# Variance products in groups of four slots, a ring of 18 slots of units, and sums and later layers one slot later, in a fused graph-network kernel

## The chip, the cores and the metric

The kernel runs on one core of a Trainium2 chip, in one launch. The metric is the time of the launch on the device in microseconds (us). Lower is better. Three runs of the kernel before took 2769.07, 2771.56 and 2772.95 us.

The core has a matrix engine (PE, whose weight loads the profile lists as PEld), a vector engine (DVE, VectorE), an activation engine (ACT, ScalarE), a general engine (POOL, GpSimd) and a queue engine that starts DMAs (SP). They run side by side and meet only at semaphores.

## The reference, cut to what matters

64 independent graphs of 128 nodes with 128 features go through four layers. All numbers are float32. Nearly all the work is layer 0, which makes a hidden vector for each of the 128 x 128 pairs of nodes:

```
hi = x @ W1[:H];  hj = x @ W1[H:]
h = relu(hi[:, None, :] + hj[None, :, :] + b1)      # 128 x 128 pairs, 128 numbers each
y = h @ W2 + b2
y = (y - mean(y)) / sqrt(var(y) + 1e-5) * gamma + beta
out[i] = sum over j of adj[i, j] * y[i, j]
```

The later layers (a normalized graph convolution, a sum with a two-matrix network, and three convolutions with layer norms) work on one 128x128 matrix per graph, each a product or two and a norm.

## The kernel before

**Layer 0.** A unit is 128 pairs: h for one i, features on the partitions, j along the free dimension. Eight units are a slot's worth (`DUO_UNITS`), and a graph has 16 of them (`SLOTS`). A slot's worth t goes through these steps:

- hidden (L547, L662, L917): the eight units `relu(v + u_i)`, shared out over three engines. DVE makes unit 0 where t is odd (four units where t is 15), POOL the last two or three, ACT what is between.
- products (L403): two PE products of 128x512 with the centred W2, into one of two halves of `y_ps`. The first needs units 0 to 3 and, through `sq_done`, that the half is free; the second needs the rest.
- squares (L565): ACT reads both halves' 1024 columns, squares them and writes `sq`, a ring of `SQ_RING` = 4 slots.
- variances (L419): PE sums squares over the features. A product with a shifted one-column selector (`sel`) writes 32 rows of `ss_ps`, and four such products (q = 0 to 3, two slots' worth of two blocks) go to four groups of 32 columns of the array.
- deviations (L569): once per half graph (eight slots' worth) ACT takes the square root of `ss_ps`. SP straightens it into `devs` with four narrow DMAs, DVE inverts it and multiplies it into the adjacency (`invert` L689, `coefficients` L694), SP stores that to DRAM and reads it back spread over the partitions (`cb`).
- weighted sums (L673): DVE multiplies each unit of h by its coefficients and sums, eight per slot's worth. The buffer `h` holds 16 slots' worth, and a hidden step waits until the sum 16 slots earlier is done (`ttr_done`).

**The order.** It is written by hand. Every engine runs an endless pipeline of iterations (one per graph) of 16 slots, and in slot s it works on the slot's worth s minus a lag:

```
hidden: s - START (START = 4)        products: s - (START + 1)
squares: s - (START + 2)             variances: s - (START + 3), at odd s
deviations: START + HALF + 2 = 14    invert, coefficients: START + HALF + 3 = 15
weighted sums: first half of the eight at s - TTR_LAG = s - 18, second at s - 19
```

So in slot n PE multiplies n-5, while ACT first squares n-6 and then makes the units of n-4. PE's order in a slot is: first product, later-layer steps of places 0 to 3, second product, later-layer steps of places 4 to 8, variance products. ACT's is: square, deviations where due, later-layer steps of places 1 to 3, units (with steps of places 4 to 7 after the second and the fourth unit), the rest. POOL makes its last unit a slot ahead (`EARLY_AT`), and makes three units in the slots of `ROOTLESS`, those in which no root of a norm falls on it.

**Later layers.** The table `AT` (L88) gives each step of the later layers a slot and a place within it. The steps of a graph are spread over some 29 slots behind its layer 0, in the iterations of the next graphs (`tails`). SP's order per iteration stands in `iteration` (L361), and each of its waits holds up what is behind it.

Of the kernel before, what the change touches and what calls it, by code (L numbers as in the profile page):

```python
# [20 lines left out]
START = 4  # L21
TTR_LAG = START + 14
TAIL_LAG = START + 28
LAYERS = 3
SQ_RING = 4
ROOTLESS = (1, 2, 4, 6, 8, 10, 13, 15)
SPAN = P // 2
# [60 lines left out]
for _name, _slot, _fine in [  # L88
    ("adj_turn", 0, 0), ("adj_turned", 0, 6), ("row_sum", 0, 2), ("degree", 0, 5), ("has_degree", 1, 5),
    ("c_sum_mm", 1, 4), ("c_sum", 1, 8), ("x_base", 2, 3),  # L90
# [9 lines left out]
]:  # L100
    place(_name, _slot, _fine)


def build(nc, x, adj, nodemask, l0_W1, l0_b1, l0_W2, l0_b2, l0_gamma, l0_beta, l1_W, l1_b,
# [4 lines left out]
    with ExitStack() as ctx:  # L109
# [39 lines left out]
        uT, vT = sb("uT", [P, 2, P]), sb("vT", [P, 2, P])  # L149
        h = sb("h", [P, SLOTS, DUO_UNITS * P])  # L150
        sq = sb("sq", [P, SQ_RING, DUO_UNITS * P])
# [125 lines left out]
        def _(sp):  # L277
# [83 lines left out]
            def iteration(after, graphs, buf):  # L361
                new, old, older, oldest = graphs
                if old is not None:
                    spread_coefficients(old, 0)
                if after is not None:
                    wait_apart(sp, x_turned, new + 1)
                    wait_apart(sp, x_in_in, 16 * (new + 1))
                    sp.dma_start(x_in[:], x[after]).then_inc(x_in_in, 16)
                if old is not None:
                    straighten_deviations(old, 1)  # L370
                    store_coefficients(old, 1)
                    spread_coefficients(old, 1)
                    if new is not None:
                        load_adj_c(new)
                    load_tail(old, 1 - buf)
                if oldest is not None:
                    wait_apart(sp, normed["ln3"], oldest + 1)
                    wait_apart(sp, out_stored, 16 * oldest)
                    sp.dma_start(out[oldest], x4[:, 1 - buf, :]).then_inc(out_stored, 16)
                if new is not None:  # L380
                    straighten_deviations(new, 0)
                    store_coefficients(new, 0)
# [5 lines left out]
        def _(pe):  # L388
# [15 lines left out]
            def products(g, t, block_of_duo):  # L404
# [10 lines left out]
                c0 = block_of_duo * COLS  # L415
                op = pe.matmul(y_ps[:, t % 2, c0:c0 + COLS], w2c[:], h[:, t, c0:c0 + COLS], start=True, stop=True)  # L416
                if block_of_duo == 1:
                    op.then_inc(y_done, 1)

            def variances(g, t):  # L420

                half, p = t // HALF, (t % HALF) // 2
                wait(pe, sq_done, SLOTS * g + t + 2)
                if p == 0:
                    wait(pe, dev_done, 2 * g + half)
                for q in range(4):
                    c0 = (q % 2) * COLS
                    mm = pe.matmul(ss_ps[32 * q:32 * q + 32, :], sel[:, ROWS - 1 - p:ROWS - 1 - p + 32],  # L428
                                   sq[:, (t + q // 2) % SQ_RING, c0:c0 + COLS],
                                   start=(p == 0), stop=(p == ROWS - 1))  # L430
                mm.then_inc(var_summed, 1)
# [75 lines left out]
            def iteration(after, graphs, buf):  # L507
                new = graphs[0]
                for s in range(SLOTS):
# [11 lines left out]
                    for g, b, place in tails(graphs, buf, s):  # L521
                        later_layers(g, b, place + 4, place + FINE)
                    if s == 11 and after is not None:
                        turn_x(after, 1 - buf)
                    sg, t = lagging(graphs, s, START + 3)
                    if s % 2 == 1 and sg is not None:
                        variances(sg, t)
# [4 lines left out]
        def _(act):  # L532
# [14 lines left out]
            def hidden(g, b, t, n):  # L547

                if n == vector_units(g, t):
                    wait(act, ttr_done, SLOTS * (g - 1) + t + 1)  # L550
                    if t == 0:
                        wait(act, uv_ready, g + 1)
                i = unit_of(t, n)
                v = v_ps if t < SLOTS - 1 else vT[:, b, :]
                op = act.activation(h[:, t, n * P:(n + 1) * P], v, ACT.Relu, bias=uT[:, b, i:i + 1])  # L555
                if n == BLOCK_UNITS - 1:
# [4 lines left out]
            def squares(g, t):  # L561

                wait(act, y_done, SLOTS * g + t + 1)
                wait(act, var_summed, SLOTS // 2 * g + (t - SQ_RING) // 2 + 1)
                act.activation(sq[:, t % SQ_RING, :], y_ps[:, t % 2, :], ACT.Square,  # L565
                               bias=b2c_col[:], scale=float(P) ** -0.5).then_inc(sq_done, 1)

            def deviations(g, half):

                wait(act, var_summed, SLOTS // 2 * g + HALF // 2 * (half + 1))  # L570
                wait(act, devs_in[half], 64 * g)
# [44 lines left out]
            def iteration(after, graphs, buf):  # L616
                new = graphs[0]
                for s in range(SLOTS):
# [31 lines left out]
                    if act_end(hg, ht) <= first + 4:  # L650
                        tail_steps(6, 8)
                    if s == 12 and after is not None:
                        keep_xT(after, 1 - buf)
# [5 lines left out]
        def _(dve):  # L659
            def hidden(g, b, t, n):  # L660

                if n == 0:  # L662
                    wait(dve, ttr_done, SLOTS * (g - 1) + t + 1)
                    if t <= 1:
                        wait(dve, uv_ready, g + 1)

                i = unit_of(t, n)
                op = dve.tensor_scalar(h[:, t, n * P:(n + 1) * P], vT[:, b, :], uT[:, b, i:i + 1], 0.0, ALU.add, ALU.max)  # L668
                if n == vector_units(g, t) - 1:
                    op.then_inc(h_dve, 1)  # L670

            def weighted_sum(g, t, n):

                if n == 0:
# [4 lines left out]
                    if t == 0:  # L679
# [3 lines left out]
                c0 = (t % 2) * DUO_UNITS * P + n * P  # L683
                op = dve.tensor_tensor_reduce(h[:, t, cols], h[:, t, cols], cb[:, t // 2, c0:c0 + P],  # L684
                                              1.0, 0.0, ALU.mult, ALU.add, gT[:, i:i + 1])
# [187 lines left out]
        def _(pool):  # L873
# [43 lines left out]
            def hidden(g, b, t, n):  # L917

                wait(pool, ttr_done, SLOTS * (g - 1) + t + 1)
                if t == 0:  # L920
                    wait(pool, uv_ready, g + 1)
                i = unit_of(t, n)
                op = pool.tensor_scalar(h[:, t, n * P:(n + 1) * P], vT[:, b, :], uT[:, b, i:i + 1], 0.0, ALU.add, ALU.max)  # L923
                if n == DUO_UNITS - 1:
# [44 lines left out]
```

## Time and profile before

| what | value |
|---|---|
| median of the runs shown | 2771.56 us (2769.07 to 2772.95) |
| profiled execution, its own time | 2773.57 us |
| its span, first to last instruction | 2772.0 us |
| mean granted clock of PE | 0.989 of full speed |
| PE busy | 2707.0 us, 98% |
| DVE busy | 2618.7 us, 94% |
| ACT busy | 2565.2 us, 93% |
| POOL busy | 2491.0 us, 90% |
| DMA | mean 206 GB/s, queue busy 54.5% |

How to read it. The times of one profiled execution are set against its own time, which is 1.6 us above its span. Engines overlap, so busy shares do not add up. A product shows as two passes (MATMUL rows "x2"), each with a weight load (LDWEIGHTS). Matmuls are pipelined and their ends are modelled, so starts are compared with starts, and a row's length is longer than its distance to the next row. The timeline merges neighbours of one kind into one row: its columns are start, length, engine, line, operation, and in brackets the idle time of the engine before it with what ended it. "issue" is time in which nothing in the profile was waited for.

### The profile page before, as it was taken

The page shows a single profiled execution, that of the slowest core. Times are in us where ns is not written, and L with a number is a line of the kernel's source. Part 1 is how long each engine was busy: PE and PEld are TensorE (multiplying, and loading weights), DVE is VectorE, ACT ScalarE, POOL GpSimd, SP SyncE. Part 2 cuts the span into 40 slices and gives each one's busy share as a digit, 9 for nine tenths or more (in the row PEclk, how much of TensorE's full clock was granted, in tenths as well). Part 3 has the DMA queues.
Part 4 walks back from the last instruction along what each step waited for, and adds up shares of the span by engine and source line. Part 5 has one row for each costly group of instructions (what it writes and reads, how often), then busy time and mean ns, then how long its engine had stood idle before and what let it go on. Part 6 is the DMA issues. An engine that isn't in the chain of part 4 may idle for free.

```text
span 2772.0 us, 60903 instructions
## 1 busy us (share of the span) xinstructions
PE 2707.0 (98%) x10882; PEld 1128.4 (41%) x10882; DVE 2618.7 (94%) x20102; ACT 2565.2 (93%) x6903; POOL 2491.0 (90%) x3498
## 2 busy tenths in 40 slices
PE   8999999999999999999999999999999999999993
PEld 2344444444444444444444444444444444444442
DVE  4999999999999999999999999999999999999997
ACT  7999999999999999999999999999999999999991
POOL 3899999999999999999999999999999989999992
PEclk9999999999999999999999999999999999999995
DMA  3655655655555555556556555555555565465552
GB/s 104 239 195 211 234 198 197 230 215 192 214 226 202 204 216 222 195 213 234 195 198 235 209 192 227 223 193 210 226 207 195 205 234 203 192 228 222 193 214 108
DMA packets 188668, 571.72 MB, mean 206 GB/s; under 512 B 70656, under 2 KB 106368, under 8 KB 139136
## 3 DMA queue, kind: packets, MB, share of 16 engines
q1 hardware_dynamic: 188288, 567.83, 54.5%
q14 instruction: 285, 2.33, 0.2%
q8 instruction: 95, 1.56, 0.2%
HBM read 555.17 MB, written 8.39 MB: 203 GB/s over the span
## 4 chain that ended last, share of the span: by engine, by line
PE 59%; DVE 13%; ACT 11%; DMA 10%; issue 5%; SPq 2%; POOL 0%; DVEq 0%; POOLq 0%; ACTq 0%
PE y_ps L416 41%; PE ss_ps L428 11%; DVE h L684 8%; ACT h L555 6%; DMA cb<-c_scratch 6%; ACT sq L565 3%; DMA c_scratch<-c 2%; DMA devs<-dev_rows 2%; SPq L324 1%; ACT dev_rows L572 1%; PE prod_bank L478 1%; PE prod_bank L482 1%; DVE h L668 1%; DVE stats L708 1%; DVE gT L684 1%
## 5 line engine op out<-in xcount | busy, mean ns | idle before, releaser
L923 POOL TENSOR_SCALAR h<-vT,uT 128x128 f32<-128x128 f32 x2520 | 2063.8, 834 | 54.1 <-ACT vT L545 44.6
L684 DVE CUSTOM_DVE_ANT_0 h<-h,cb 128x128 f32<-128x128 f32 x8192 | 2005.8, 291 | 74.4 <-DMA cb<-c_scratch 71.4
L416 PE MATMUL y_ps<-h,w2c 128*128 128x512 f32 x4096 | 2032.8, 613 | 11.9 <-DVE h L668 2.8
L555 ACT ACTIVATE h<-uv_ps,uT 128x128 f32<-128x128 f32 x4785 | 1426.9, 441 | 0.0
L565 ACT ACTIVATE sq<-y_ps,b2c_col 128x1024 f32<-128x1024 f32 x1024 | 1193.5, 1166 | 139.3 <-PE y_ps L416 138.6
L416 PEld LDWEIGHTS y_ps<-h,w2c 128*128 128x128 f32 x4096 | 672.9, 190 | 944.1 <-issue 647.3
L684 DVE DVE_READ_ACCUMULATOR2_ANT gT<- 128x1 f32 x8192 | 637.5, 78 | 0.0
L428 PE MATMUL ss_ps<-sq,sel 128*32 128x512 f32 x4096 | 545.5, 605 | 0.8 <-ACT sq L565 0.8
L914 POOL TENSOR_TENSOR rs<-var_eps,minus_half 128x1 f32<-128x1 f32 x448 | 297.9, 665 | 35.1
L911 POOL TENSOR_TENSOR var_eps<-mv,eps_col 128x1 f32<-128x1 f32 x448 | 94.8, 212 | 132.7 <-DVE mv L711 129.2
L668 DVE TENSOR_SCALAR h<-vT,uT 128x128 f32<-128x128 f32 x757 | 202.1, 295 | 4.7 <-ACT mask_all L610 2.6
L428 PEld LDWEIGHTS ss_ps<-sq,sel 128*32 128x32 f32 x4096 | 80.6, 108 | 247.8 <-ACT sq L565 141.2
L708 DVE BATCH_NORM_STATS2 stats<-z 128x6 f32<-128x128 f32 x448 | 127.1, 284 | 0.3
L482 PEld LDWEIGHTS prod_bank<-l3w,aggT 128*128 128x128 f32 x384 | 73.4, 193 | 93.3 <-issue 73.0
L692 DVE RECIPROCAL invs<-devs 128x64 f32<-128x64 f32 x128 | 70.2, 548 | 38.4 <-DMA devs<-dev_rows 36.7
L717 DVE TENSOR_SCALAR x<-z,mv,rs 128x128 f32<-128x128 f32 x256 | 96.7, 378 | 6.1 <-POOL rs L914 4.8
L603 ACT ACTIVATE h<-z_aff 128x128 f32<-128x128 f32 x192 | 75.7, 394 | 19.0 <-DVE z_aff L791 19.0
L711 DVE BATCH_NORM_AGGREGATE mv<-stats 128x2 f32<-128x6 f32 x448 | 78.4, 175 | 4.7
L572 ACT ACTIVATE dev_rows<-ss_ps 128x512 f32<-128x512 f32 x128 | 79.6, 622 | 1.2 <-PE ss_ps L428 1.2
L598 ACT ACTIVATE aggT<-prod_bank 128x128 f32<-128x128 f32 x192 | 61.6, 321 | 20.6 <-PE prod_bank L478 20.6
L482 PE MATMUL prod_bank<-l3w,aggT 128*128 128x128 f32 x384 | 76.3, 281 | 2.6 <-ACT aggT L598 2.6
L791 DVE SCALAR_TENSOR_TENSOR z_aff<-z_aff,rs,l3beta 128x128 f32<-128x128 f32 x192 | 75.0, 391 | 3.0 <-POOL rs L914 3.0
(100 smaller groups left out, 1460.6 us busy)
## 6 DMA issues: line engine op xcount, KB each, us to landing
cb<-c_scratch SPq DMA_DIRECT2D x384, 1024.0 KB, 9.4
cb<-c_scratch SPq DMA_DIRECT2D x256, 512.0 KB, 4.9
adj_c<-in_adj_dram SPq DMA_DIRECT2D x512, 8.0 KB
devs<-dev_rows SPq DMA_DIRECT2D x512, 8.0 KB
x_in<-in_x_dram SPq DMA_DIRECT2D x64, 64.0 KB, 10.9
c_scratch<-c SPq DMA_DIRECT2D x128, 32.0 KB, 1.5
adj_in<-in_adj_dram SPq DMA_DIRECT2D x64, 64.0 KB, 4.4
x_res<-in_x_dram SPq DMA_DIRECT2D x64, 64.0 KB, 5.3
```

The costliest lines, as they stand in the source:

```text
L416: op = pe.matmul(y_ps[:, t % 2, c0:c0 + COLS], w2c[:], h[:, t, c0:c0 + COLS], start=True, stop=True)
L428: mm = pe.matmul(ss_ps[32 * q:32 * q + 32, :], sel[:, ROWS - 1 - p:ROWS - 1 - p + 32], sq[:, (t + q // 2) % SQ_RING, c0:c0 + COLS], start= ...
L482: pe.matmul(out, aggT[:, b, :], l3w[:, i, :], start=True, stop=False)
L555: op = act.activation(h[:, t, n * P:(n + 1) * P], v, ACT.Relu, bias=uT[:, b, i:i + 1])
L565: act.activation(sq[:, t % SQ_RING, :], y_ps[:, t % 2, :], ACT.Square, bias=b2c_col[:], scale=float(P) ** -0.5).then_inc(sq_done, 1)
L572: act.activation(dev_rows[:, half, :], ss_ps[:], ACT.Sqrt, bias=EPS).then_inc(dev_done, 1)
L668: op = dve.tensor_scalar(h[:, t, n * P:(n + 1) * P], vT[:, b, :], uT[:, b, i:i + 1], 0.0, ALU.add, ALU.max)
L684: op = dve.tensor_tensor_reduce(h[:, t, cols], h[:, t, cols], cb[:, t // 2, c0:c0 + P], 1.0, 0.0, ALU.mult, ALU.add, gT[:, i:i + 1])
L708: dve.bn_stats(stats[:, b, :], z[:, b, :]).then_inc(stats_set[name], 1)
L717: dve.tensor_scalar(dst[:, b, :], z[:, b, :], mv[:, b, 0:1], rs[:, b:b + 1], ALU.subtract, ALU.mult).then_inc(normed[name], 1)
L914: pool.tensor_tensor(rs[:, b:b + 1], var_eps[:, b:b + 1], minus_half[:], ALU.pow).then_inc(rs_set[name], 1)
L923: op = pool.tensor_scalar(h[:, t, n * P:(n + 1) * P], vT[:, b, :], uT[:, b, i:i + 1], 0.0, ALU.add, ALU.max)
```

## The change

Four things change together.

- A variance step takes four slots' worth (`GROUP` = 4), eight products instead of four, and stands in slots 1, 5, 9 and 13 instead of in every odd slot. The ring of squares goes from 4 to 6, and the waits on `var_summed` count groups of four.
- `h` becomes a ring of 18 slots' worth (`H_RING`), and the weighted sums come one slot later (`TTR_LAG` = START + 15). A hidden step waits for the sum 18 slots earlier.
- All steps of the later layers from `g_keep` on, the transposition of the next x and its copy are placed one slot later. `ROOTLESS`, the slots in which POOL makes three units, follows the places of the roots.
- SP starts the narrow DMAs of the first half's deviations before the store of the output instead of after it.

```diff
-TTR_LAG = START + 14
-TAIL_LAG = START + 28
+TTR_LAG = START + 15
+H_RING = 18
 LAYERS = 3
-SQ_RING = 4
-ROOTLESS = (1, 2, 4, 6, 8, 10, 13, 15)
+SQ_RING = 6
+GROUP = 4
+ROOTLESS = (1, 2, 3, 5, 7, 9, 11, 14)
...
-    ("g_keep", 2, 4), ("l0_mm", 3, 0), ("l0_sum", 3, 5), ("ln0", 3, 6), ("x1_scaled", 4, 6),
-    ("l1_agg", 5, 0), ("l1_agg_keep", 5, 8), ("l1_mm", 6, 0), ("l1_bias", 6, 7), ("l1_relu", 7, 0),
+    ("g_keep", 3, 4), ("l0_mm", 4, 0), ("l0_sum", 4, 5), ("ln0", 4, 6), ("x1_scaled", 5, 6),
+    ("l1_agg", 6, 0), ("l1_agg_keep", 6, 8), ("l1_mm", 7, 0), ("l1_bias", 7, 7), ("l1_relu", 8, 0),
...
-    ("l3_relu2", 26, 6), ("final_sum", 28, 2), ("ln3", 28, 3),
+    ("l3_relu2", 27, 6), ("final_sum", 29, 2), ("ln3", 29, 3),
...
-        h = sb("h", [P, SLOTS, DUO_UNITS * P])
+        h = sb("h", [P, H_RING, DUO_UNITS * P])
...
+                if new is not None:
+                    straighten_deviations(new, 0)
                 if oldest is not None:
                     wait_apart(sp, normed["ln3"], oldest + 1)
                     wait_apart(sp, out_stored, 16 * oldest)
                     sp.dma_start(out[oldest], x4[:, 1 - buf, :]).then_inc(out_stored, 16)
                 if new is not None:
-                    straighten_deviations(new, 0)
                     store_coefficients(new, 0)
...
             def variances(g, t):
 
-                half, p = t // HALF, (t % HALF) // 2
-                wait(pe, sq_done, SLOTS * g + t + 2)
-                if p == 0:
+                half = t // HALF
+                wait(pe, sq_done, SLOTS * g + t + GROUP)
+                if t % HALF == 0:
                     wait(pe, dev_done, 2 * g + half)
-                for q in range(4):
-                    c0 = (q % 2) * COLS
-                    mm = pe.matmul(ss_ps[32 * q:32 * q + 32, :], sel[:, ROWS - 1 - p:ROWS - 1 - p + 32],
-                                   sq[:, (t + q // 2) % SQ_RING, c0:c0 + COLS],
-                                   start=(p == 0), stop=(p == ROWS - 1))
+                for d in range(GROUP):
+                    p = (t + d) % HALF // 2
+                    for block in range(2):
+                        q = 2 * (d % 2) + block
+                        mm = pe.matmul(ss_ps[32 * q:32 * q + 32, :], sel[:, ROWS - 1 - p:ROWS - 1 - p + 32],
+                                       sq[:, (SLOTS * g + t + d) % SQ_RING, block * COLS:(block + 1) * COLS],
+                                       start=(p == 0), stop=(p == ROWS - 1))
                 mm.then_inc(var_summed, 1)
...
-                    if s == 11 and after is not None:
+                    if s == 12 and after is not None:
                         turn_x(after, 1 - buf)
-                    sg, t = lagging(graphs, s, START + 3)
-                    if s % 2 == 1 and sg is not None:
+                    sg, t = lagging(graphs, s, START + 1 + GROUP)
+                    if t % GROUP == 0 and sg is not None:
                         variances(sg, t)
...
-                    wait(act, ttr_done, SLOTS * (g - 1) + t + 1)
+                    wait(act, ttr_done, SLOTS * g + t - H_RING + 1)
...
-                wait(act, var_summed, SLOTS // 2 * g + (t - SQ_RING) // 2 + 1)
-                act.activation(sq[:, t % SQ_RING, :], y_ps[:, t % 2, :], ACT.Square,
+                wait(act, var_summed, (SLOTS * g + t - SQ_RING) // GROUP + 1)
+                act.activation(sq[:, (SLOTS * g + t) % SQ_RING, :], y_ps[:, t % 2, :], ACT.Square,
...
-                    if s == 12 and after is not None:
+                    if s == 13 and after is not None:
                         keep_xT(after, 1 - buf)
```

The index of `h` becomes `(SLOTS * g + t) % H_RING` wherever it is read or written, and DVE's and POOL's hidden steps wait as ACT's does.

**PE, from the round of slot 5 to that of slot 7 in the steady stretch, before.** The names: y_ps are layer 0's products (two per slot), ss_ps the variance products, prod_bank the later layers. The first row is the round of slot 5, the last the round of slot 7.

```order
L428 MATMUL ss_ps<-sq,sel 32x512 x4
L416 MATMUL y_ps<-h,w2c 128x512
L463 MATMUL prod_bank<-l1wT,aggT 128x128
L416 MATMUL y_ps<-h,w2c 128x512 x2
L478 MATMUL prod_bank<-adj_in,h 128x128
L416 MATMUL y_ps<-h,w2c 128x512
L428 MATMUL ss_ps<-sq,sel 32x512 x4
```

The same place in the changed kernel, from the round of slot 5 towards that of slot 9:

```order
L432 MATMUL ss_ps<-sq,sel 32x512 x8
L418 MATMUL y_ps<-h,w2c 128x512
L464 MATMUL prod_bank<-adjT,x1s 128x128
L418 MATMUL y_ps<-h,w2c 128x512 x2
L467 MATMUL prod_bank<-l1wT,aggT 128x128
L418 MATMUL y_ps<-h,w2c 128x512 x2
L482 MATMUL prod_bank<-adj_in,h 128x128
L418 MATMUL y_ps<-h,w2c 128x512 x2
L486 MATMUL prod_bank<-l3w,aggT 128x128
L487 MATMUL prod_bank<-bias_parts,pick 128x128
```

Before, four layer 0 products lie between two rounds. After, eight do, with the later layers' products of four slots between them (the last layer 0 product, the two products of l2_agg and the round follow the listing).

**SP, from the narrow loads of one graph to the store of its first coefficients, before.**

```order
L288 DMA adj_c<-in_adj_dram 32x1x64 x8
L358 DMA adj_in<-in_adj_dram 128x128
L359 DMA x_res<-in_x_dram 128x128
L379 DMA out_dram<-x 128x128
L324 DMA devs<-dev_rows 32x1x64 x4
L335 DMA c_scratch<-c 128x64
```

And after:

```order
L289 DMA adj_c<-in_adj_dram 32x1x64 x8
L359 DMA adj_in<-in_adj_dram 128x128
L360 DMA x_res<-in_x_dram 128x128
L325 DMA devs<-dev_rows 32x1x64 x4
L382 DMA out_dram<-x 128x128
L336 DMA c_scratch<-c 128x64
```

The output's store now stands between the deviations' narrow DMAs and the store of the coefficients made from them.

## Rows read from the trace of the kernel before

**Rows 1.** The page: busy time by engine, and shares of the last chain.
```profile
PE 2707.0 (98%) x10882; PEld 1128.4 (41%) x10882; DVE 2618.7 (94%) x20102; ACT 2565.2 (93%) x6903; POOL 2491.0 (90%) x3498
PE 59%; DVE 13%; ACT 11%; DMA 10%; issue 5%; SPq 2%; POOL 0%; DVEq 0%; POOLq 0%; ACTq 0%
```

**Rows 2.** Timeline of PE, the row of L401 in two graphs.
```profile
298.39 0.38 PE L401 MATMUL uv_ps<-xT,w1a 128*128 128x128 f32 x2
...
2365.55 0.39 PE L401 MATMUL uv_ps<-xT,w1a 128*128 128x128 f32 x2
```

**Rows 3.** Timeline of PE from 1399.5 us.
```profile
1399.52 1.02 PE L416 MATMUL y_ps<-h,w2c 128*128 128x512 f32 x2
1400.38 0.38 PE L460 MATMUL prod_bank<-adjT,x1s 128*128 128x128 f32 x2
1400.60 1.02 PE L416 MATMUL y_ps<-h,w2c 128*128 128x512 f32 x2
1401.55 1.07 PE L428 MATMUL ss_ps<-sq,sel 128*32 128x512 f32 x8
1402.55 1.12 PE L416 MATMUL y_ps<-h,w2c 128*128 128x512 f32 x2
1403.51 0.38 PE L463 MATMUL prod_bank<-l1wT,aggT 128*128 128x128 f32 x2
```

**Rows 4.** Timeline of PE, the four small passes ahead of a round.
```profile
1390.19 0.50 PE L449 MATMUL prod_bank<-rows_sum,row_pick 128*128 128x1 f32 x4
1390.63 1.07 PE L428 MATMUL ss_ps<-sq,sel 128*32 128x512 f32 x8
```

**Rows 5.** Timeline of PE, the product that waited for ACT, and one later.
```profile
1404.87 1.12 PE L416 MATMUL y_ps<-h,w2c 128*128 128x512 f32 x2
1405.83 0.38 PE L478 MATMUL prod_bank<-adj_in,h 128*128 128x128 f32 x2
...
1408.96 0.39 PE L482 MATMUL prod_bank<-l3w,aggT 128*128 128x128 f32 x2
1409.18 0.22 PE L483 MATMUL prod_bank<-bias_parts,pick 96*128 96x128 bf16 x1
1409.24 1.07 PE L416 MATMUL y_ps<-h,w2c 128*128 128x512 f32 x2
1410.15 0.38 PE L466 MATMUL prod_bank<-adj_in,x 128*128 128x128 f32 x2
```

**Rows 6.** Timeline of ACT over the same stretch.
```profile
1403.13 0.65 ACT L572 ACTIVATE dev_rows<-ss_ps 128x512 f32<-128x512 f32 x1
1403.61 1.20 ACT L555 ACTIVATE h<-uv_ps,uT 128x128 f32<-128x128 f32 x4
...
1405.06 1.22 ACT L565 ACTIVATE sq<-y_ps,b2c_col 128x1024 f32<-128x1024 f32 x1
1406.05 1.51 ACT L555 ACTIVATE h<-uv_ps,uT 128x128 f32<-128x128 f32 x5
1407.30 0.43 ACT L598 ACTIVATE aggT<-prod_bank 128x128 f32<-128x128 f32 x1
...
1410.36 1.11 ACT L565 ACTIVATE sq<-y_ps,b2c_col 128x1024 f32<-128x1024 f32 x1 [0.34 <-PE y_ps L416]
```

**Rows 7.** Timeline of PE's weight loads: a round, and the product that waited.
```profile
1401.55 0.16 PEld L428 LDWEIGHTS ss_ps<-sq,sel 128*32 128x32 f32 x8 [0.76 <-ACT sq L565]
...
1404.86 0.30 PEld L416 LDWEIGHTS y_ps<-h,w2c 128*128 128x128 f32 x2 [0.94 <-ACT h L555]
```

**Rows 8.** Waits by engine and line: us in total, times, longest us.
```profile
PEld y_ps L416 <- ACT h L555: 198.3, 383, 1.5
...
PEld y_ps L416 <- DVE h L668: 81.0, 93, 1.9
...
DVE h L684 <- DMA cb<-c_scratch: 71.4, 116, 2.7
...
DVE invs L692 <- DMA devs<-dev_rows: 36.7, 48, 19.8
```

More of the change, by code:

```diff
@@ L415, in products @@
                 c0 = block_of_duo * COLS
-                op = pe.matmul(y_ps[:, t % 2, c0:c0 + COLS], w2c[:], h[:, t, c0:c0 + COLS], start=True, stop=True)
+                op = pe.matmul(y_ps[:, t % 2, c0:c0 + COLS], w2c[:], h[:, (SLOTS * g + t) % H_RING, c0:c0 + COLS], start=True, stop=True)
                 if block_of_duo == 1:
@@ L554, in hidden @@
                 v = v_ps if t < SLOTS - 1 else vT[:, b, :]
-                op = act.activation(h[:, t, n * P:(n + 1) * P], v, ACT.Relu, bias=uT[:, b, i:i + 1])
+                op = act.activation(h[:, (SLOTS * g + t) % H_RING, n * P:(n + 1) * P], v, ACT.Relu, bias=uT[:, b, i:i + 1])
                 if n == BLOCK_UNITS - 1:
@@ L563, in squares @@
                 wait(act, y_done, SLOTS * g + t + 1)
-                wait(act, var_summed, SLOTS // 2 * g + (t - SQ_RING) // 2 + 1)
-                act.activation(sq[:, t % SQ_RING, :], y_ps[:, t % 2, :], ACT.Square,
+                wait(act, var_summed, (SLOTS * g + t - SQ_RING) // GROUP + 1)
+                act.activation(sq[:, (SLOTS * g + t) % SQ_RING, :], y_ps[:, t % 2, :], ACT.Square,
                                bias=b2c_col[:], scale=float(P) ** -0.5).then_inc(sq_done, 1)
             def deviations(g, half):
-                wait(act, var_summed, SLOTS // 2 * g + HALF // 2 * (half + 1))
+                wait(act, var_summed, SLOTS // GROUP * g + HALF // GROUP * (half + 1))
                 wait(act, devs_in[half], 64 * g)
@@ L662, in hidden @@
                 if n == 0:
-                    wait(dve, ttr_done, SLOTS * (g - 1) + t + 1)
+                    wait(dve, ttr_done, SLOTS * g + t - H_RING + 1)
                     if t <= 1:
@@ L667, in hidden @@
                 i = unit_of(t, n)
-                op = dve.tensor_scalar(h[:, t, n * P:(n + 1) * P], vT[:, b, :], uT[:, b, i:i + 1], 0.0, ALU.add, ALU.max)
+                op = dve.tensor_scalar(h[:, (SLOTS * g + t) % H_RING, n * P:(n + 1) * P], vT[:, b, :], uT[:, b, i:i + 1], 0.0, ALU.add, ALU.max)
                 if n == vector_units(g, t) - 1:
@@ L683, in weighted_sum @@
                 c0 = (t % 2) * DUO_UNITS * P + n * P
-                op = dve.tensor_tensor_reduce(h[:, t, cols], h[:, t, cols], cb[:, t // 2, c0:c0 + P],
+                op = dve.tensor_tensor_reduce(h[:, (SLOTS * g + t) % H_RING, cols], h[:, (SLOTS * g + t) % H_RING, cols], cb[:, t // 2, c0:c0 + P],
                                               1.0, 0.0, ALU.mult, ALU.add, gT[:, i:i + 1])
@@ L917, in hidden @@
             def hidden(g, b, t, n):
-                wait(pool, ttr_done, SLOTS * (g - 1) + t + 1)
+                wait(pool, ttr_done, SLOTS * g + t - H_RING + 1)
                 if t == 0:
@@ L922, in hidden @@
                 i = unit_of(t, n)
-                op = pool.tensor_scalar(h[:, t, n * P:(n + 1) * P], vT[:, b, :], uT[:, b, i:i + 1], 0.0, ALU.add, ALU.max)
+                op = pool.tensor_scalar(h[:, (SLOTS * g + t) % H_RING, n * P:(n + 1) * P], vT[:, b, :], uT[:, b, i:i + 1], 0.0, ALU.add, ALU.max)
                 if n == DUO_UNITS - 1:
```

12 rows, old and new, of the table AT are left out of this document.

## The prediction

> **What bounds the kernel now.** I read the page first [rows 1]. Four engines are busy for 90 to 98% of the span, so no busy share names the bound, and the chain of waits puts 59% on PE. The period comes next. PE makes u and v (L401) once per graph, and two such rows 49 graphs apart give (2365.55 - 298.39) / 49 = 42.19 us per graph [rows 2]. The 64 graphs make 2700 us of it; the rest is filling and draining.
>
> Then PE's timeline [rows 3]. A 128x512 product is two passes. From L416 at 1399.52 to L460 at 1400.38 is 0.86, so a pass is 0.43 and a slot's two products take 1.72. From L416 at 1400.60 to the variance products at 1401.55 is 0.95, 0.09 more than two passes. A round of four variance products lasts 1.00 to the next product, and that product takes 0.96, again 0.10 more. A round costs 0.09 + 1.00 + 0.10 = 1.19 us, and it stands after every second slot: eight per graph. A 128x128 product costs 0.22 (L460 to L416), l3w with its bias product 0.28 (1408.96 to 1409.24), and the four small L449 passes 0.35, being 0.44 less the entry's 0.09 [rows 3 to 5].
>
> Last, how PE and ACT hold each other. PE's slot n makes the product of unit-slot n-5, while ACT in slot n squares n-6 and then makes units of n-4. The second last pass of a product begins at 1409.24 and its last 0.43 before L466 at 1410.15, at 1409.72; the waiting square starts at 1410.36, 0.64 later [rows 5, 6]. From the square at 1405.06 to the next ACT unit is 0.99, and five units take 1.25, 0.25 each [rows 6]. The units that start at 1403.61 have their fourth at 1404.36, and the product that waited for it starts at 1404.87, 0.50 later; its weight loads stand at the same moment with "ACT h" behind them, and it takes 0.96 to the next row, 0.10 more than a stream [rows 5 to 7].
>
> So there is a two-slot loop. With P(n) the start of PE's slot n and A(n) the start of ACT's square: A(n) is at least P(n-1) + 1.29 + 0.63 = P(n-1) + 1.92 plus what stands between the two products, and P(n+1) is at least A(n) + 1.01 + three pitches 0.75 + 0.50 = A(n) + 2.26. In odd slots VectorE makes the first unit, and it is A(n) + 2.01. The loop is **3.9 to 4.2 us over two slots**, and small ACT steps or a late ACT come on top. Of the 42.19, 16 x 1.72 and 8 x 1.19 are products and rounds; 5.2 is left for later layers and waits, about 0.3 per slot. So PE without a round needs 2.0 a slot, while ACT needs 1.0 + four to six units at 0.25 + small steps, 2.0 to 2.7. Today every two slots hold one round and last 5.2, which covers both the loop and ACT nearly everywhere; PE waits for ACT's units at one slot, 1404.87, behind the deviations at 1403.13 [rows 6, 7].
>
> **The change part by part.** *Groups of four.* Four rounds of eight replace eight rounds of four. The same products are made, and a round of eight has four streams of passes in place of two. In a round of four, 1.00 is the last pass with its change (0.52, as 0.95 less 0.43) and 0.48 for the first four passes [rows 3]. Two more streams cost 0.86 to 0.96; I take 0.90. A round of eight is then 0.09 + 1.90 + 0.10 = 2.09, against 2.38 for two rounds: **PE has 0.29 less per pair, 256 x 0.29 = 74 us over the kernel.** The bounds: nothing, if each further stream pays entry and exit again (0.19 + 0.10 and the stagger), and 0.33.
>
> The weight loads could take that gain. All eight loads of a round start within 0.16 us of its beginning, though its passes last 1.00 [rows 7], so loads for the second stream lie under the first, and I charge none. The Trainium skill, "TensorE: Matmul & The Clock Gate", section "What overlaps and what doesn't", says weight loads overlap running matmuls only when their row groups differ; here all four tiles use all 128 rows, so by it each further stream would pay its load. At the loads' 0.11 that would be 0.21 per round of eight, 54 us over the kernel. The trace speaks against that rule for this form, and the sum goes without it.
>
> *Where the cover goes.* Rounds now stand behind slots 1, 5, 9 and 13 only. I step P and A through a graph; a product behind a round or a wait takes 1.82. Slots 6 to 9, with P(6) = 0: round 5 has just ended. ACT squared long ago, but its deviations need the round's last pass (0.52 earlier, seen 0.63 after its start), so they begin at 0.11 and take 0.48 [rows 6]. Six units and a copy follow, and A(7) = 2.25. P(7) = 1.82 + 0.22 = 2.04, no wait. P(8) by PE would be 3.98, but A(7) + 2.01 = 4.26. A(8) = 2.25 + ACT's slot 7 (1.0 + four units 1.0 + 0.2) = 4.45, so P(9) is 6.71 where PE by itself says 4.26 + 1.82 + 0.22 = 6.30. Then P(10) = 6.71 + 1.82 + later layers 0.73 + the round's 1.99 = 11.25. By the same steps slots 10 to 13 take 10.76 (waits at 12 and 13), slots 14 to 1 take 10.68 (waits at 0 and 1) and slots 2 to 5 take 10.44 (nearly no wait, since slot 3's later-layer work has moved to slot 4). **The sum is 43.13 us per graph, 0.94 above today's 42.19.** PE's work falls by 4 x 0.29 = 1.2, but some six waits a graph take its place, 0.2 to 0.5 each with 0.10 behind them. Over 64 graphs that is +60 us.
>
> *Ring of 18, sums one slot later.* VectorE waits 71.4 us for coefficients (cb) and 36.7 for deviations [rows 1, 8]. One slot more removes most of the first. That is worth nothing on the path: VectorE is ahead of PE, which waited 81.0 us at its weight loads for VectorE's units [rows 8], nearly all of it under running passes. Without this step the cover would be the 1.5% that VectorE is idle. The ring frees buffers one slot earlier, which no engine on the path waits for.
>
> *Later layers one slot later, POOL's three-unit slots moved.* The same number of instructions on each engine. ACT's units go from five and five to six and four in slots 4 to 11. Only the first four decide P, so this costs nothing there. The last graph ends one slot later: +2 us.
>
> *SP.* The eight narrow copies and the stores are as many as before. The out store, now behind the first half's deviations, waits for ln3, due two slots before the coefficients that SP stores next. Nothing, with those two slots as the cover.
>
> The profiled execution took 2773.6, two above the median 2771.6. **2773.6 + 60 + 2 = 2836 us.**
>
> **Rivals.** *A, the loop does not bind and PE decides.* For it: PE is busy 98% and its chain share is the largest. Against it: the wait at 1404.87 is of just this kind. It would hold if units were ready earlier than my A(n) says, by 0.5 us in the slots without a round. Then the 74 us come: 2773.6 - 74 + 2 = 2702, slower turned into faster. If the waits take half of what I say the gain is eaten: about 2770. *B, VectorE with its DMA waits is the bound today.* Its busy time and those waits make 2618.7 + 71.4 + 36.7 = 2727 of 2772 [rows 1, 8]; the later sums would return about 70 us, 2705. Against it: the unit waits of PE hide under passes. *C, each further stream pays the change again*: 256 x 0.29 come on top, a little less where PE waits anyway: about 2900. The Trainium skill, "TensorEngine Tiling (Array Packing)", section "Key Properties", says only a change of tiling mode drains the engine; by that C would not happen. *D, the sizes of the waits are right but ACT's slack returns half of them elsewhere*, about 2800. *E, nothing measurable*: gain and waits cancel.
>
> **How the numbers follow.** This kernel's measurement tells about 0.2% from no change. The forecast with D and C has 0.66 (all slower), A and B 0.24 (most of it faster), E 0.10 spread to both sides. From these: faster 0.26, same 0.08, slower 0.66. The range goes from 2745, which takes in the half-gains of A, to 2870, between forecast and C. The likeliest case by itself reaches 2805 to 2860.
>
> **What would show it.** Right: the L416 starts of slots 8, 9, 12, 13, 0 and 1 stand behind ACT's fourth unit by 0.50; weight-load waits on "ACT h" rise from 198 us to over 400; a round from first variance pass to next product is near 1.9; ACT's deviations wait for the round; VectorE's cb wait nearly vanishes; the period is near 43.1. Wrong: the period is under 42, or the product starts follow each other by 1.7 to 2.0 without waits.

## The result, and the profile after

The changed kernel takes 2838.35 us, the median of four runs (2838.01 to 2839.12), where before takes 2771.64. The ratio is 1.0242, with a 95% interval from 1.0224 to 1.026: slower by 67 us. The prediction was 2836 us in a range of 2745 to 2870.

The page of the profiled execution, whose span is 2837.5 us, beside [rows 1]. First the busy times, then the shares of the chain that ended last:

```profile
PE 2695.6 (95%) x10882; PEld 1163.6 (41%) x10882; DVE 2616.5 (92%) x20102; ACT 2557.3 (90%) x6903; POOL 2487.3 (88%) x3498
...
PE 57%; ACT 32%; issue 9%; DVE 2%; POOL 0%; DMA 0%; SPq 0%; ACTq 0%; POOLq 0%; DVEq 0%
```

The instruction counts are the same, and no engine is busier but for PE's weight loads, 1163.6 us against 1128.4, which run beside its passes. The added time is idle time: the shares of PE, VectorE, ACT and POOL all fall. The chain shows who holds whom. ACT's part rises from 11% to 32%, and VectorE's and the DMAs' parts, 13% and 10% before, fall to 2% and 0%.

PE's timeline of the changed kernel, one row of L403 (u and v) in two graphs, answers to [rows 2]:

```profile
307.10 0.39 PE L403 MATMUL uv_ps<-xT,w1a 128*128 128x128 f32 x2
...
2379.49 0.38 PE L403 MATMUL uv_ps<-xT,w1a 128*128 128x128 f32 x2
```

That is 48 graphs, (2379.49 - 307.10) / 48 = 43.17 us each, against 42.19: 0.98 more, 63 us over 64 graphs.

PE's timeline from the end of slot 5 to slot 10, the stretch that the prediction stepped through, to be read beside [rows 3, 5]:

```profile
1392.41 1.92 PE L432 MATMUL ss_ps<-sq,sel 128*32 128x512 f32 x16
1394.27 1.12 PE L418 MATMUL y_ps<-h,w2c 128*128 128x512 f32 x2
1395.23 0.38 PE L464 MATMUL prod_bank<-adjT,x1s 128*128 128x128 f32 x2
1395.45 1.88 PE L418 MATMUL y_ps<-h,w2c 128*128 128x512 f32 x4
1397.17 0.38 PE L467 MATMUL prod_bank<-l1wT,aggT 128*128 128x128 f32 x2
1397.39 1.02 PE L418 MATMUL y_ps<-h,w2c 128*128 128x512 f32 x2
1398.59 1.10 PE L418 MATMUL y_ps<-h,w2c 128*128 128x512 f32 x2 [0.17 <-issue]
...
1401.03 1.12 PE L418 MATMUL y_ps<-h,w2c 128*128 128x512 f32 x2 [0.27 <-ACT h L559]
...
1405.58 1.98 PE L418 MATMUL y_ps<-h,w2c 128*128 128x512 f32 x4
```

The round lasts 1.86 from its first pass to the next product. Slot 6 starts at 1394.27, slot 7 at 1396.31 (two passes into the row at 1395.45), slot 8 at 1398.59, slot 9 at 1401.03, slot 10 at 1405.58. Slot 8's product comes 1.20 after two passes began at 1397.39, where a stream would have 0.86; slot 9's comes 1.29 after those at 1399.74.

ACT's timeline of the same stretch, beside [rows 6]:

```profile
1394.40 0.60 ACT L576 ACTIVATE dev_rows<-ss_ps 128x512 f32<-128x512 f32 x1 [0.57 <-PE ss_ps L432]
1394.89 1.65 ACT L559 ACTIVATE h<-uv_ps,uT 128x128 f32<-128x128 f32 x6
...
1396.55 1.17 ACT L569 ACTIVATE sq<-y_ps,b2c_col 128x1024 f32<-128x1024 f32 x1
1397.54 1.20 ACT L559 ACTIVATE h<-uv_ps,uT 128x128 f32<-128x128 f32 x4
...
1398.74 1.21 ACT L569 ACTIVATE sq<-y_ps,b2c_col 128x1024 f32<-128x1024 f32 x1
1399.74 1.76 ACT L559 ACTIVATE h<-uv_ps,uT 128x128 f32<-128x128 f32 x6
```

In slot 8 the third unit of the four starts at 1398.04, and PE's product 0.55 later, at 1398.59. In slot 9 the fourth unit starts at 1400.49, and the product 0.54 later, at 1401.03. PE is held by ACT's units, which stand behind a square.

The waits by engine and line (us in total, times, longest), beside [rows 8]:

```profile
PEld y_ps L418 <- ACT h L559: 325.4, 454, 1.7
...
PE y_ps L418 <- ACT h L559: 70.0, 193, 0.9
PEld y_ps L418 <- DVE h L672: 57.1, 68, 1.9
DVE invs L696 <- DMA devs<-dev_rows: 56.5, 63, 20.1
...
ACT dev_rows L576 <- PE ss_ps L432: 50.4, 126, 2.0
```

PE's waits for ACT's units, at weight loads and passes together, doubled from 200 to 395 us. The wait for cb, 71.4 us before, is no longer among the waits. ACT's deviations now wait for the long round, 126 times of 128.

One name in this list misleads. The 57.1 us of PE's loads for VectorE's unit are nearly all one wait per graph, at slot 0:

```profile
1420.32 0.30 PEld L418 LDWEIGHTS y_ps<-h,w2c 128*128 128x128 f32 x2 [0.83 <-DVE h L672]
1419.20 0.27 DVE L672 TENSOR_SCALAR h<-vT,uT 128x128 f32<-128x128 f32 x1
1419.32 1.45 ACT L559 ACTIVATE h<-uv_ps,uT 128x128 f32<-128x128 f32 x5
```

VectorE's unit had been done for 0.85 us when the product started. ACT's third unit, the last that this product needs beside VectorE's one, starts at 1419.82, and the product 0.50 later. The step is that of the other slots, so this wait too is for ACT.

### The profile page after: what moved, and what is told of

It is laid out like the page before. It is cut to its first block, busy times and chain, and to the rows that moved or that the text cites. A ratio compares the mean times of both kernels' runs of the same rounds, so it can differ in the third digit from the quotient of the medians.

```text
span 2837.5 us, 60834 instructions
## 1 busy us (share of the span) xinstructions
PE 2695.6 (95%) x10882; PEld 1163.6 (41%) x10882; DVE 2616.5 (92%) x20102; ACT 2557.3 (90%) x6903; POOL 2487.3 (88%) x3498
## 4 chain that ended last, share of the span: by engine, by line
PE 57%; ACT 32%; issue 9%; DVE 2%; POOL 0%; DMA 0%; SPq 0%; ACTq 0%; POOLq 0%; DVEq 0%
PE y_ps L418 34%; ACT h L559 20%; PE ss_ps L432 17%; ACT sq L569 10%; DVE h L688 1%; PE prod_bank L482 1%; PE prod_bank L486 1%; ACT h L607 1%; ACT hid L598 1%; PE prod_bank L453 1%; ACT aggT L602 1%; PE prod_bank L470 1%; PE uv_ps L403 1%; PE prod_bank L471 1%; PE uv_ps L404 1%
## 5 line engine op out<-in xcount | busy, mean ns | idle before, releaser
L559 ACT ACTIVATE h<-uv_ps,uT 128x128 f32<-128x128 f32 x4848 | 1443.3, 466 | 0.0
L569 ACT ACTIVATE sq<-y_ps,b2c_col 128x1024 f32<-128x1024 f32 x1024 | 1230.1, 1201 | 162.1 <-PE y_ps L418 162.1
L432 PE MATMUL ss_ps<-sq,sel 128*32 128x512 f32 x4096 | 492.5, 598 | 0.9 <-ACT sq L569 0.9
L432 PEld LDWEIGHTS ss_ps<-sq,sel 128*32 128x32 f32 x4096 | 106.9, 109 | 221.8 <-issue 154.0
L782 DVE TENSOR_TENSOR z<-prod_bank,x 128x128 f32<-128x128 f32 x64 | 18.7, 291 | 85.8 <-PE prod_bank L487 85.7
L910 POOL TENSOR_TENSOR dis_raw<-degree_floor,minus_half 128x1 f32<-128x1 f32 x64 | 35.1, 548 | 65.7 <-DVE degree_floor L736 65.7
L795 DVE SCALAR_TENSOR_TENSOR z_aff<-z_aff,rs,l3beta 128x128 f32<-128x128 f32 x192 | 83.7, 436 | 4.6 <-POOL rs L918 2.9
```

The costliest lines, as they stand in the source:

```text
L559: op = act.activation(h[:, (SLOTS * g + t) % H_RING, n * P:(n + 1) * P], v, ACT.Relu, bias=uT[:, b, i:i + 1])
L569: act.activation(sq[:, (SLOTS * g + t) % SQ_RING, :], y_ps[:, t % 2, :], ACT.Square, bias=b2c_col[:], scale=float(P) ** -0.5).then_inc(sq_ ...
```

## The experiments

Each ran beside runs of before on the same chip. Ratios are to before, with their 95% interval. A group of four slots is a round of eight products; a round of four products is that of two slots, `GROUP = 2`, as before the change.

**1. Groups of four alone.** The changed kernel with ring, sums, places, ROOTLESS and SP's order as before:

```diff
-TTR_LAG = START + 15
-H_RING = 18
+TTR_LAG = START + 14
+H_RING = 16
-ROOTLESS = (1, 2, 3, 5, 7, 9, 11, 14)
+ROOTLESS = (1, 2, 4, 6, 8, 10, 13, 15)
...
-    ("g_keep", 3, 4), ("l0_mm", 4, 0), ("l0_sum", 4, 5), ("ln0", 4, 6), ("x1_scaled", 5, 6),
+    ("g_keep", 2, 4), ("l0_mm", 3, 0), ("l0_sum", 3, 5), ("ln0", 3, 6), ("x1_scaled", 4, 6),
...
```

> Groups of four alone: the ring of squares at 6, everything else (ring of 16 units' slots, sums, later layers, ROOTLESS, SP's order) as before. Theory (the loop of square, units and product over two slots, whose cover was the round taken out of slots 3, 7, 11 and 15): nearly the whole loss is here, 2825 to 2850 us. Rival, the loss comes from the ring, the later sums or the moved later layers: 2700 to 2775 here. Rival, VectorE with its DMA waits bounds: the waits for cb stay at 70 us or grow, and this kernel is slower than the change by some 70 us, about 2905.

Measured: 2849.5 us, ratio 1.0275 (1.0257 to 1.0292). The groups alone cost 78 us, more than the whole change. The wait for cb is 62.8 us there, so it did not grow, and the kernel is far from the 2905 us of that rival. The lateness is a gain of about 11 us here, not a cost.

**2. Everything but the groups.** The changed kernel with `GROUP = 2` and `SQ_RING = 4`.

> Everything of the change but the groups: a variance round behind every second slot (GROUP = 2, SQ_RING = 4), ring of 18, sums and later layers one slot later. Theory: no difference from before that matters, 2763 to 2782 us, although VectorE's wait for cb (71 us) goes. Rival, VectorE bounds: about 2705. Rival, lateness or POOL's moved units cost the time: 2800 to 2838.

Measured: 2755.2 us, ratio 0.9936 (0.9921 to 0.9951), 16 us faster than before. This missed all three expectations: it is below the theory's range and far above the VectorE rival. Between this kernel and the change stand the groups alone, and they cost 83 us. Its waits:

```profile
PEld y_ps L418 <- ACT h L559: 158.9, 451, 1.6
...
DVE invs L696 <- DMA devs<-dev_rows: 36.9, 48, 19.3
```

**3. One slot between the units and what follows them.** In the changed kernel products, squares, variances, deviations and coefficients move one slot back, while the units stay:

```diff
+APART = 1
...
-                    yg, t = lagging(graphs, s, START + 1)
+                    yg, t = lagging(graphs, s, START + 1 + APART)
...
-                    sg, t = lagging(graphs, s, START + 1 + GROUP)
+                    sg, t = lagging(graphs, s, START + 1 + GROUP + APART)
...
-                    sg, t = lagging(graphs, s, START + 2)
+                    sg, t = lagging(graphs, s, START + 2 + APART)
...
-                    vg, t = lagging(graphs, s, START + HALF + 2)
+                    vg, t = lagging(graphs, s, START + HALF + 2 + APART)
...
-                    cg, ct = lagging(graphs, s, START + HALF + 3)
+                    cg, ct = lagging(graphs, s, START + HALF + 3 + APART)
```

> The change, with products, squares, variances, deviations and coefficients one slot later than the units (hidden steps stay), so that PE's product no longer needs units that ACT makes in the slot just before it, behind a square: the loop gets three slots instead of two. No instruction is added or taken away. Theory: PE's waits (3.4 us per graph in the changed kernel, 0.4 of it restarts behind rounds) go, PE would need 40.2 us per graph, VectorE needs 40.7, so 40.7 to 41.9 per graph: 2680 to 2755 us, the upper end if the waits for cb return, since coefficients are now made one slot later against the sums. Rival, a round of eight costs as much as two of four, or PE's products run slower for another reason than this loop: 2800 to 2838.

Measured: 2774.3 us, ratio 1.0011 (1.0002 to 1.002). Against the changed kernel 64 us come back, without an instruction more or less. It is 19 us above the range I gave. Its waits show where the gain is from and what is left:

```profile
PEld prod_bank L487 <- ACT aggT L603: 172.0, 190, 1.4
...
ACT uT L549 <- PE uv_ps L405: 62.8, 64, 2.7
...
PEld y_ps L419 <- ACT h L560: 18.9, 79, 0.2
```

The products' wait for ACT's units falls from 395 to 19 us. In its place stand later-layer steps that were placed for the old distance between PE and ACT.

**4. The same distance with rounds of four** (`GROUP = 2`, `SQ_RING = 4` in experiment 3).

> As the kernel with everything one slot apart, but with a round behind every second slot (GROUP = 2, SQ_RING = 4). Theory: the loop was nearly covered there, so only PE's 0.6 us of real waits per graph can go: 2730 to 2770 us, and slower than the groups of four in the same setting by 10 to 74 us (4 x 0.29 us per graph where PE bounds both). Rival, groups of four save PE nothing: the same time as the groups of four in this setting, or less.

Measured: 2765.5 us, ratio 0.9979 (0.9966 to 0.9991). The time is in the range, but the comparison went to the rival's side: rounds of four are 9 us faster here. The extra slot makes the kernel with rounds of four 10 us slower (experiment 2 took 2755.2) and the one with groups of four 64 us faster, so it gives back something that only the groups had lost. The penalty of the groups is down from 83 to 9 us, and what was left of it could be the misplaced steps: PE waits 204 us for aggT (L603) in experiment 3 and 36 here.

**5. Three placements mended.** Experiment 3 with:

```diff
-    ("l3_agg0", 13, 4), ("l3_agg_keep0", 14, 2), ("l3_mm0", 14, 4), ("l3_sum0", 15, 2),
-    ("l3_ln0", 15, 3), ("l3_relu0", 17, 2), ("l3_agg1", 20, 0), ("l3_agg_keep1", 20, 8),
+    ("l3_agg0", 13, 4), ("l3_agg_keep0", 14, 2), ("l3_mm0", 15, 0), ("l3_sum0", 15, 6),
+    ("l3_ln0", 15, 7), ("l3_relu0", 17, 2), ("l3_agg1", 20, 0), ("l3_agg_keep1", 20, 8),
-    ("l3_agg2", 24, 0), ("l3_agg_keep2", 24, 8), ("l3_mm2", 25, 0), ("l3_sum2", 26, 1), ("l3_ln2", 26, 2),
+    ("l3_agg2", 24, 0), ("l3_agg_keep2", 24, 8), ("l3_mm2", 25, 4), ("l3_sum2", 26, 1), ("l3_ln2", 26, 2),
...
+                    if s == START - 1 and new is not None:
+                        make_uv(new)
                     if yg is not None:
                         products(yg, t, 0)
-                    if s == START - 1 and new is not None:
-                        make_uv(new)
```

> Groups of four with products and what follows one slot after the units, and three steps of the hand-written order moved to where they no longer wait: u and v are made ahead of the first product of slot 3, the product with the first matrix of the last layer stands in the middle of slot 15 (its sum and norm behind it), and that with the third at the end of slot 9. If the waits left in the untuned kernel are those placements alone (1.1 us per graph of PE for ACT's aggT, 0.9 of ACT for PE's u and v), PE needs 40.3 us per graph and VectorE 40.7, so 41.0 to 41.7: 2700 to 2745 us. Rival, once the loop is open another limit of about 42 holds (VectorE with its DMA waits): 2765 to 2775.

Measured: 2747.3 us, ratio 0.9921 (0.9904 to 0.9937). This is **faster than both kernels**, by 24 us than before and by 91 than the change, and the lowest median of all. Its four runs spread from 2744.8 to 2755.2, though, and those of experiment 2 lie at 2754.6 to 2755.8, so its 8 us over that kernel are not established. It is 2 us above the range. The waits that the three moves aimed at fall, PE's for aggT (L603) from 204 to 36 us and ACT's for PE's u and v from 63 to 4. The moves were not tried one by one. Page and waits, from its slowest run:

```profile
PE 2643.0 (96%) x10882; PEld 1160.8 (42%) x10882; DVE 2627.5 (95%) x20102; ACT 2564.1 (93%) x6903; POOL 2545.0 (92%) x3498
```

```profile
PEld ss_ps L433 <- ACT sq L570: 178.9, 184, 1.2
...
PEld y_ps L419 <- ACT h L560: 27.0, 113, 0.2
```

Now PE's rounds wait for ACT's squares, and the four engines stand within four points of each other, at 92 to 96%.

**6. The same placements with rounds of four.**

> The same placements with a round behind every second slot. PE's own work with eight rounds is 41.6 us per graph: 2740 to 2760 us, and slower than the groups of four in the same setting by 10 to 55 us. Rival, the groups of four save PE nothing once the loop is open: equal.

Measured: 2769.6 us, ratio 0.9992 (0.9982 to 1.0001), 10 us above its range. In this setting the groups of four are 22 us faster, within the expected 10 to 55. So the sign of the grouping depends on what covers ACT: +83 us with the two-slot loop, +9 with the loop open, -22 with the placements fitted to it. The last comparison favours the groups, since the placements were chosen on their kernel: rounds of four lose 4 us by them against experiment 4. The wait of ACT for u and v falls with them too, from 51 to 3 us, but PE's rounds wait longer for the squares, 209 us against 164. Set against the best kernel with rounds of four, experiment 2, the groups gain 8 us by the medians.

**7. Of the lateness only the later layers' places** (with `ROOTLESS` and SP's order, which go with them). Experiment 2 with the sums and the ring as before:

```diff
-TTR_LAG = START + 15
-H_RING = 18
+TTR_LAG = START + 14
+H_RING = 16
...
-    ("g_keep", 3, 4), ("l0_mm", 4, 0), ("l0_sum", 4, 5), ("ln0", 4, 6), ("x1_scaled", 5, 6),
+    ("g_keep", 2, 4), ("l0_mm", 4, 0), ("l0_sum", 4, 5), ("ln0", 4, 6), ("x1_scaled", 5, 6),
```

> Of the kernel with lateness but no groups, only the later layers' places (and ROOTLESS, and SP's order) are kept: sums at START + 14, ring of 16, g_keep at its old place, rounds of four. If the 16 us that lateness gave came from the later layers' places (the relu that stood with the deviations in ACT's slot 6, and slot 3's 1.1 us of PE work, were moved apart): 2752 to 2762 us, with VectorE's wait for cb still there. Rival, they came from the ring and the later sums: 2768 to 2776.

Measured: 2757.7 us, ratio 0.9954 (0.9939 to 0.9969). The places, with `ROOTLESS` and SP's order, give 13 of the 16 us. The ring and the later sums give the last 2.5, or 5 by the ratios, whose intervals overlap, although they take away VectorE's whole wait for cb. It is, in this kernel:

```profile
DVE h L688 <- DMA cb<-c_scratch: 45.2, 88, 2.2
```

and in experiment 2:

```profile
DVE h L688 <- DMA cb<-c_scratch: 0.2, 1, 0.2
```

**8. The round half a slot later**, between the two products of the next slot, in experiment 5's kernel:

```diff
+                    sg, st = lagging(graphs, s, START + 2 + GROUP + APART)
+                    if st % GROUP == 0 and sg is not None:
+                        variances(sg, st)
                     if yg is not None:
                         products(yg, t, 1)
...
-                    sg, t = lagging(graphs, s, START + 1 + GROUP + APART)
-                    if t % GROUP == 0 and sg is not None:
-                        variances(sg, t)
```

> As the tuned kernel with groups of four, but the round stands between the two products of the next slot instead of at the end of its own, 0.9 us later, because there PE waited 0.9 us per graph for ACT's squares (at the rounds and at the product behind them). The same number of rounds. If that wait was lateness of ACT by less than one product, 0.3 to 0.7 us per graph come back: 2700 to 2730 us, against 2747. Rival, the deviations of the half graph, which now wait 0.9 us longer for the round, hold ACT and eat it: 2740 to 2765 us.

Measured: 2984.6 us, ratio 1.077 (1.0752 to 1.0788). A clear miss: the rival had the direction and less than a tenth of the size. Its waits:

```profile
DVE invs L697 <- DMA devs<-dev_rows: 176.3, 127, 2.4
ACT dev_rows L577 <- PE ss_ps L433: 156.7, 127, 2.5
...
PE uv_ps L404 <- ACT h L560: 96.9, 62, 1.6
```

ACT's deviations stand in a slot whose round now comes behind PE's next product, so ACT stops in front of its units each time:

```profile
1421.60 0.60 ACT L577 ACTIVATE dev_rows<-ss_ps 128x512 f32<-128x512 f32 x1 [1.46 <-PE ss_ps L433]
1422.09 1.13 ACT L560 ACTIVATE h<-uv_ps,uT 128x128 f32<-128x128 f32 x4
...
1443.26 0.60 ACT L577 ACTIVATE dev_rows<-ss_ps 128x512 f32<-128x512 f32 x1 [0.98 <-PE ss_ps L433]
1443.75 1.39 ACT L560 ACTIVATE h<-uv_ps,uT 128x128 f32<-128x128 f32 x5
```

That is the first explanation, which experiment 10 tests. The units behind are four and five here, not the six that its expectation names.

**9. Deviations behind the units, in the changed kernel.** The three lines of `deviations` in ACT's slot move from in front of the units to behind them.

> The changed kernel with ACT's deviations behind the units of their slot instead of ahead of them (nothing else). The trace of the change has ACT waiting 50 us there for the round of eight, which is new. Theory by the stepped slots: the square of slot 7 is set by PE's product (2.24 after the round), not by ACT's own work, whether the deviations stand ahead or behind, so that wait lies off the path: no change against the changed kernel, 2830 to 2843 us. Rival, ACT's wait for the round is part of the loss: 2785 to 2815.

Measured: 2847.4 us, ratio 1.0279 (1.0263 to 1.0294): 9 us slower than the change, 4 above the range. ACT's wait for the round goes from 50 to 2 us, and nothing comes back. PE's waits for ACT's units fall by 31 us, to 365, while the loads that the profile puts down to VectorE's units rise from 57 to 158 and VectorE's wait for the deviations from 57 to 115. So the move shifts waits and costs a little on balance; that the wait for the round was no part of the loss is not shown by it alone.

**10. The same move in experiment 8's kernel.**

> The kernel with the round between two products (2985 us) with the deviations behind the units of their slot. If the 157 us of ACT's waits for the round there, ahead of six units that PE needs, made that kernel slow, the placing now shows what it was meant to: 2700 to 2745 us. Rival, PE's squares and the norms' steps being a slot out of place make it slow by themselves: over 2850.

Measured: 2937.2 us, ratio 1.0603 (1.0585 to 1.062). ACT's wait for the round drops from 157 to 32 us, and only 47 of the 237 us over experiment 5 come back. What this kernel keeps of its waits:

```profile
DVE invs L697 <- DMA devs<-dev_rows: 175.1, 126, 2.5
...
PE uv_ps L404 <- ACT h L560: 96.5, 62, 1.6
```

So the first explanation of experiment 8 holds for a fifth of it. The rest is still open. These two waits are candidates that neither kernel lost (VectorE's for the deviations is 3.7 us in experiment 5), and so is PE's for aggT (L592), 108 and 106 us.

**11. The same move in experiment 5's kernel.**

> The tuned kernel of groups of four (2747 us) with the deviations behind the units. ACT waits for the round only 0.1 us per graph there, but its units come 0.5 us earlier twice per graph. Expected: 2735 to 2750 us, a little faster if the units' place mattered; slower (2750 to 2765) if the coefficients' DMAs, now 1.3 us later, are what VectorE waits for.

Measured: 2809.9 us, ratio 1.0147 (1.013 to 1.0163): 63 us slower than experiment 5, in the direction of the second case but over three times its size. VectorE waits more for the deviations (3.7 us in experiment 5), and PE for a norm that VectorE finishes late:

```profile
PEld prod_bank L465 <- DVE x1s L763: 86.7, 64, 2.5
DVE invs L697 <- DMA devs<-dev_rows: 67.0, 73, 2.0
```

In experiment 5 PEld's wait for x1s is 39.7 us. In the chain that ended last VectorE and the DMAs have 23% and 10% here, against 14% and 7% there. This points to the path from the deviations over DMAs and VectorE back to PE, which had its share in the chain of the kernel before as well (13% and 10%) [rows 1]; no run isolates it.

## Why the prediction was right, point by point

**PE bounds, in a loop with ACT: right.** Experiment 3 is the test. The same instructions with one slot more between units and products are 64 us faster, and the wait for units goes from 395 to 19 us. With rounds of four the same step gains nothing (experiments 2 and 4). A rival that blames the round's price or PE's passes cannot explain that, since both stay as they are; nor can VectorE, whose coefficients come a slot later there and whose wait for cb returns (29.6 us). Rival A is out with it, and rivals D (about 2800) and E (no change) by the time.

**The price of a round.** The prediction took 0.09 + 1.90 + 0.10 = 2.09. The trace shows 1.86 and the same entry and restart, 2.05. Against two rounds of 1.19 that saves 0.33, not 0.29, so the two further streams cost 0.43 each, the low end. Rival C, each stream paying the change again, is out. So is the sum by the Trainium skill, "TensorE: Matmul & The Clock Gate", section "What overlaps and what doesn't", with loads not overlapping for lack of different row groups: it would add 0.21 to the round, and nothing was added to the two further streams beyond their passes of 0.43.

**The stepped slots.** Predicted starts against measured, from the start of slot 6:

| | predicted | measured |
|---|---|---|
| ACT's deviations | 0.11 | 0.13 |
| P(7) | 2.04 | 2.04 |
| A(7) | 2.25 | 2.28 |
| P(8) | 4.26 | 4.32 |
| A(8) | 4.45 | 4.47 |
| P(9) | 6.71 | 6.76 |
| P(10) | 11.25 | 11.31 |

P(14) follows at 1416.28 and P(2) at 1426.96 in this trace:

```profile
1416.28 1.98 PE L418 MATMUL y_ps<-h,w2c 128*128 128x512 f32 x4
...
1422.85 1.98 PE L418 MATMUL y_ps<-h,w2c 128*128 128x512 f32 x4 [0.44 <-ACT h L559]
...
1426.96 2.84 PE L418 MATMUL y_ps<-h,w2c 128*128 128x512 f32 x6
```

Slots 10 to 13 took 10.70 (10.76 predicted) and slots 14 to 1 took 10.68 (10.68). The period was predicted at 43.13 and measured at 43.17. The six waits stand where the prediction put them, before slots 8, 9, 12, 13, 0 and 1. The step from the last needed unit to the product is 0.48 to 0.55 in them, 0.52 on average, not 0.50. The errors are small, and the saved 0.04 of the round partly offsets them. The 2 us for the last graph also came out: outside its 64 periods the kernel before spends 73.6 us (2773.57 less 64 x 42.187) and the changed one 75.9 (2839.12 less 64 x 43.175).

**Where the sum hid an error.** The prediction said that moving the later layers costs nothing and that the ring is worth nothing on the path. The ring was nearly right, 2.5 us. The places were not: they give 13 us. The absolute period came out right because the stepping used the new places, but the text credited no term with it. The groups themselves cost 83 us, not 60. What the places took away can be seen at slot 7. In the kernel before PE has a wait there, 0.38 us with its restart (four passes from 1403.73 to 1405.83); in experiment 2 it has none (four passes from 1394.44 to 1396.16). ACT's slots 5 and 6, before and then in experiment 2:

```profile
1400.73 1.39 ACT L555 ACTIVATE h<-uv_ps,uT 128x128 f32<-128x128 f32 x5
1401.98 0.31 ACT L587 ACTIVATE aggT<-prod_bank 128x128 f32<-128x128 f32 x1
...
1404.61 0.40 ACT L603 ACTIVATE h<-z_aff 128x128 f32<-128x128 f32 x1
```

```profile
1391.33 1.13 ACT L559 ACTIVATE h<-uv_ps,uT 128x128 f32<-128x128 f32 x4
1392.37 1.11 ACT L569 ACTIVATE sq<-y_ps,b2c_col 128x1024 f32<-128x1024 f32 x1
```

Expected of experiment 7 was the relu (L603) beside the deviations of slot 6. It starts at 1404.61, behind the fourth unit of 1404.36, so it did not hold that product. What ACT has less of is in slot 5: four units where there were five, since POOL now makes three, and no copy of aggT, some 0.4 us together. That is a reading of one period. Which move gave the 13 us was not tried alone, and experiment 2 has a new wait of about the same size before slot 15.

**VectorE.** Rival B, VectorE with its DMA waits, is out by experiment 2: the cb wait goes and 16 us are gained, not 66. The few tenths at slot 0, which the list of waits puts down to VectorE, are ACT's as predicted (the rows in the section on the result).

**SP.** The moved store is in experiments 2 and 7 too, which are faster than before; it was not tried alone. SP waited 58 times for ln3 at it before (86.7 us) and three times after (46.9 us).

**The signs to look for** came out but for a size: weight-load waits for "ACT h" at 325 where over 400 was said (395 with the waits of the passes), the round at 1.86 ("near 1.9"), deviations waiting, the cb wait gone, the period at 43.17.

## What to carry to other kernels

When an edit removes work from a busy engine, look at what that work covered. A filler between two dependent steps can be worth more as cover than it costs, and bunching it leaves bare stretches in which the next loop binds. Write that loop as two or three inequalities from start to start, with latencies from rows where something waited, and step through one period; here it gave each start to 0.06 us. And try the saving again after giving the loop a slot more: the same grouping costs 83 us with a distance of one slot and gains 22 with two and fitted placements. Compare with the best kernel without the saving as well: here the gain over it is 8 us by the medians, which the runs do not establish.

## What the runs showed that I had not expected

A detour of PE into 32-column products costs 0.33 us on top of its streams of 0.43, for two streams and for four alike: 1.19 less 0.86 before, 2.05 less 1.72 after. It is 0.09 on the way in, 0.14 within the round (which the prediction split into 0.05 and 0.09) and 0.10 more for the first product behind it. A product that waited took 0.07 to 0.10 more too: 0.93 and 0.96 to the next row at 1398.59 and 1401.03, where a stream has 0.86. The mean granted clock was 0.99 of full speed in both kernels, so this is at the 2.4 GHz level.

In this kernel, with four engines busy over 90%, the order of a step against its neighbours mattered more than the price of a round. Moving ACT's deviations behind the units cost 9 us in one setting and 63 in another and gave 47 in a third, and moving a round by one product cost 237.
